# Key and value products on four quarter tiles of TensorE, in a four-block convolution and attention kernel

## The reference

```python
qkv = xf @ qkv_w.T + qkv_b                  # xf: (B, N, 64), N = 128*128 pixels
q, k, v = ...                               # 8 heads of 8 channels each
k = _layernorm(k, kln_w, kln_b)             # over the 8 channels of a head, std with ddof=1
v = _layernorm(v, vln_w, vln_b)
kv = einsum('bhnd,bhne->bhde', k, v) / N    # sum over all pixels
av = einsum('bhnd,bhde->bhne', q, kv)
h1 = gelu((av + x) @ o1_w.T + o1_b)
out = h1 @ o2_w.T + o2_b + x
```

## Time and profile before

| | us |
|---|---|
| median of three executions | 2690.85 (2689.84 to 2691.07) |
| profiled execution | 2696.16 |
| its span | 2694.4 |
| TensorE matmul busy | 2546.2 (95%) |
| TensorE weight loads busy | 2460.3 (91%) |
| VectorE busy | 1848.3 (69%) |
| ScalarE busy | 1220.0 (45%) |
| GpSimd busy | 171.3 (6%) |
| mean granted TensorE clock | 0.979 |

### The profile page before, as it was taken

How to read it: one execution, slowest core, us unless ns; L and a number is a source line. 1 busy time by engine, 2 the same in 40 slices (tenths; PEclk the granted TensorE clock), 3 DMA queues, 4 the chain that set the end, 5 groups by cost and what they waited for, 6 DMA issues and landing times.

```text
span 2694.4 us, 115786 instructions
## 1 busy us (share of the span) xinstructions
PE 2546.2 (95%) x45062; PEld 2460.3 (91%) x45062; DVE 1848.3 (69%) x6030; ACT 1220.0 (45%) x2531; POOL 171.3 (6%) x291
## 2 busy tenths in 40 slices
PE   1999999999999999997899999999999999978998
PEld 1299999999999999997899999999999999977985
DVE  7866666666566666678566666666666666787876
ACT  0866663222233333356666632222333333566767
POOL 1610000000000000000000000000000000002435
PEclk9999999999999999998899999999999999988999
DMA  6810001222300000024900012224000000240006
GB/s 262 223 32 0 0 0 45 60 61 59 94 0 0 0 5 0 0 65 115 368 17 0 0 38 60 62 60 101 0 0 0 0 0 0 63 110 16 3 2 250
DMA packets 158376, 146.46 MB, mean 54 GB/s; under 512 B 22497, under 2 KB 146018, under 8 KB 154210
## 3 DMA queue, kind: packets, MB, share of 16 engines
q1 hardware_dynamic: 146432, 142.65, 17.8%
q10 hardware_dynamic: 11874, 2.90, 0.5%
HBM read 61.61 MB, written 50.33 MB: 42 GB/s over the span
## 4 chain that ended last, share of the span: by engine, by line
PE 91%; DVE 3%; DMA 3%; issue 2%; SPq 1%; ACT 1%; DVEq 0%; ACTq 0%; POOL 0%
PE banks L750 82%; PE banks L804 4%; PE banks L816 1%; PE banks L723 1%; PE banks L712 1%; DMA state<-x_in 1%; PE banks L797 1%; DVE state L950 1%; DMA res<-resid 1%; SPq L265 1%; DVE state L1086 0%; DMA resid<-state 0%; DVE state L947 0%; ACTq L465 0%; DMA state<-resid 0%
## 5 line engine op out<-in xcount | busy, mean ns | idle before, releaser
L750 PE MATMUL banks<-x_row,w_taps 128*64 128x124 f32 (+2 forms) x40640 | 2207.7, 270 | 16.6 <-DVE x_row L1000 9.1
L750 PEld LDWEIGHTS banks<-x_row,w_taps 128*64 128x64 f32 x40640 | 2205.3, 135 | 18.9 <-issue 9.8
L1009 DVE SCALAR_TENSOR_TENSOR x_row<-banks,sweep_nbias,biased_row 128x128 f32<-128x128 f32 x2032 | 714.2, 351 | 723.2 <-PE banks L750 704.0
L552 ACT ACTIVATE biased_row<-state,sweep_bias 128x256 f32 (+1 forms) x762 | 511.2, 671 | 1029.3 <-DVE state L1012 594.5
L548 ACT ACTIVATE biased_row<-state,aff,gn_a 128x64 f32 (+1 forms) x1016 | 364.1, 429 | 185.1 <-DVE state L1018 185.1
L1012 DVE SCALAR_TENSOR_TENSOR state<-banks,sweep_nbias,biased_row 128x128 f32 (+1 forms) x1016 | 444.1, 437 | 0.3
L1018 DVE SCALAR_TENSOR_TENSOR turn_ring<-banks,sweep_nbias,biased_row 128x64 f32<-128x64 f32 x1016 | 237.5, 276 | 0.0
L1018 DVE SCALAR_TENSOR_TENSOR state<-banks,sweep_nbias,biased_row 128x64 f32 (+1 forms) x1016 | 237.4, 276 | 0.1
L410 POOL TENSOR_SCALAR res<-res 128x128 f32<-128x128 f32 x64 | 43.2, 675 | 2397.1 <-ACT res L661 2397.0
L804 PEld LDWEIGHTS banks<-kvw_s,state 64*128 64x128 f32 x1024 | 118.1, 308 | 0.1
L723 PE MATMUL banks<-res,ffn_w 64*64 64x512 f32 x512 | 112.3, 597 | 6.0 <-ACT res L484 5.2
(11 more groups left out here) (137 smaller groups left out, 777.0 us busy)
## 6 DMA issues: line engine op xcount, KB each, us to landing
state<-turn_ring SPq DMA_DIRECT2D x512, 64.0 KB, 1.9
state<-x_in SPq DMA_DIRECT2D x16, 1024.0 KB, 20.7
resid<-state SPq DMA_DIRECT2D x64, 256.0 KB, 3.7
res<-resid SPq DMA_DIRECT2D x16, 1024.0 KB, 9.1
res<-resid SPq DMA_DIRECT2D x32, 512.0 KB, 5.4
resid<-state SPq DMA_DIRECT2D x16, 1024.0 KB, 11.6
out_y<-state SPq DMA_DIRECT2D x16, 1024.0 KB, 4.0
state<-resid SPq DMA_DIRECT2D x32, 256.0 KB, 9.2
```

What stands on the lines that cost most here:

```text
L552: nc.scalar.activation(as_cells(n, biased_row[:, k, :, :]), cells(n, slice(0, B), i, k, g), ACT.Identity, bias=sweep_bias[:, n:n + 1]).the ...
L750: last = nc.tensor.matmul(out_ps[blk, :, lo:hi], w_taps[:, n % 2, s, blk], x_row[c][src][:, :, s + lo:s + hi], start=at == 0, stop=at == T ...
L1009: nc.vector.scalar_tensor_tensor(x_row[c][par][:, :, 2:2 + HALF], ps, nb, br, ALU.max, ALU.add).then_inc(row_ready[c], 1)
```

## The change

Each matmul of line 804 with 128 weight columns (pixels) becomes two with 64 weight columns, one for each half m of the pixels, which write partitions 0 to 63 and 64 to 127 of the same bank. With the two halves q that makes four quarter tiles of the array (64 rows x 64 columns). The moving operand, the banks, the sums, their order over t and the semaphores stay. The bias products of line 797 and everything else stay as they are. (The feed-forward before and after is the same in both kernels.)

```diff
                     for q in range(2):
                         blk = slice(q * C, (q + 1) * C)
                         col = q * BANK + t * KVN
-                        last = nc.tensor.matmul(pair[n % KV_BANKS][:, col:col + KVN], half_rows[blk, top:top + P, b, w],
-                                                kvw_s[blk, b, :], start=False, stop=t == PARTS - 1)
+                        for m in range(2):
+                            at = slice(m * C, (m + 1) * C)
+                            last = nc.tensor.matmul(pair[n % KV_BANKS][at, col:col + KVN],
+                                                    half_rows[blk, top + m * C:top + (m + 1) * C, b, w],
+                                                    kvw_s[blk, b, :], start=False, stop=t == PARTS - 1)
                 last.then_inc(kv_done, 1)
```

## The result

| | before | after |
|---|---|---|
| median, us | 2690.35 (4 executions) | 2669.02 (4 executions, 2666.94 to 2671.62) |
| ratio | | 0.9921, 95% interval 0.9904 to 0.9939 |
| profiled execution, us | 2696.16 | 2671.62 |
| its span, us | 2694.4 | 2669.8 |
| first bias load of the loop to the last reduce, us | 170.5 | 146.4 |

The change is faster by 21.3 us; 28.5 were forecast. The last row of the table cuts out the loop, from the first weight load of line 797 to the start of line 1135's last reduce, and is the cleanest measure of the change. What lies ahead of the loop is the same code in both, yet its length differs from one execution to the next: the loop started between 2437.3 and 2444.5 us in the profiles of this study. What lies behind it took 79.4 us before and 79.5 after.

What follows compares the result with a forecast made beforehand. TensorE was taken to bound the attention loop, with VectorE next at 2.185 us a tile. Gains of 28.1 us in the loop and 0.4 at start-up, 28.5 off the median 2690.85, gave 2662.4 us, range 2657 to 2676.

Steps and rivals of the forecast that it cites:

- What bounds the kernel: Attention loop: TensorE never idle for 158.4 us, 2.68 us a tile; only shortening its part moves the time.
- Why 804 was slow: Key/value products: weight loads of the two row tiles go one after the other, 0.22 us a round, about twice streaming.
- Step 1: Line 804's products: loads hide behind streaming, eight rounds of 0.099 us, 0.79 us a tile in place of 1.65.
- Step 2: Tile-shape switches between 797, 804 and 816: still two a tile, one moves; cost 0 to 0.2 us, taken as 0.
- Step 3: TensorE's tile after the change: 0.41 + 0.79 + 0.62 = 1.82 us, or 2.02 with a further switch.
- Step 4: Next bound in the loop: VectorE sets the tile at 2.185 us, TensorE waiting about 0.3 us a tile.
- that case (2668): VectorE's tile in the loop 2.26 us instead of 2.185, from a product of 0.77 for 0.69; costs 4.5 us.
- Step 5: The sum: 28.1 us from tile 6's reduce to the last, 0.4 at start-up, 0 behind the loop; 28.5 us.
- Serial loads: Rival on 804: 32 loads one after another take 1.76 us; 2691 us, or 2704 with 0.2 more a tile; 5%.
- The clock: Rival: waiting TensorE drops to clock 0.50, its tile 3.4 us; 2732 us if the whole loop ran so; 4%.
- Loads not hidden behind streaming: Rival on 804: round 0.15 us, 804 takes 1.2, TensorE's tile 2.2 to 2.43; up to 2676 us; 7%.
- the sign that was to overturn the forecast: The forecast fails altogether if TensorE's matmul row stays full over the loop.

Runs made afterwards that it cites:

- half the columns: Changed kernel with each key/value product streaming 56 of its 112 columns; round 0.147 us, one execution 2667.0 us.
- the control: The changed kernel run once more, nothing altered; 2666.99 us, ratio 0.991 to the kernel before.
- GpSimd later: Changed kernel with dense weights, GpSimd's two steps for tile n held until VectorE has scaled tile n - 2; 2662.63 us, ratio 0.9907.
- GpSimd later alone: Changed kernel with its true weights, only GpSimd's steps held until VectorE has scaled tile n - 2; 2666.82 us, ratio 0.9913.

## Why the prediction was right, and where not

**What bounds the kernel.** Right: TensorE's share of the tile was the bound, and shortening 804 moved the time. The two small engines behind it were not.

**Why 804 was slow.** Wrong in its reason. The loads were the limit, as read, but I took the earlier trace rows (lone dense loads of 0.11 us) and the earlier trace rows (pairs of 0.22) to show that loads of two row tiles are serial. The runs show that they are parallel, and that the stride of 512 bytes took the time: 0.112 us a round with dense weights in the old form. The comparison that hid it was between a lone dense tile and a strided pair; two things differed at once, and I named only one. I even wrote that the stride has no price, on that ground. The records of the kernel before held the answer: the two loads of a round start 0.003 us apart and last 0.310 us each, and the next two start 0.220 us later. The earlier trace rows shows them merged.

**Step 1, loads and streaming.** The term of the sum that was mis-sized: 0.79 us for 806 was expected, 8 x 0.147 = 1.18 measured. The interpolation itself was good: with dense weights the round is 0.096 where 0.099 was worked out, and TensorE's tile less its wait is 2.261 - 0.452 = 1.81 us where 1.82 was forecast. The gram's row was the wrong price because its weights are dense. I had the doubt in the text (four strided loads at once may have a price), gave it 7%, and put the right size (0.15) on it, but with another mechanism: half the columns show that no streaming is in these 0.147 us.

**Step 2, switches.** Right. The gap moved from the gram to 806. Measured between the same points, the way from the bias load to the second round of the products grew by 0.21 us, and that from the last round of the products to the gram's second round shrank by 0.22.

**Step 3, TensorE's tile.** 1.82 forecast, 2.24 measured: 0.39 of the difference is step 1.

**Step 4, what is late next.** Half right. VectorE is next and free of waits, as the earlier trace rows foretold at 2.185 us, but for a TensorE faster than that the tile is 2.26, since GpSimd's step then meets the product. The range had that case (2668) from the product of 0.77 in the earlier trace rows; the sum didn't. The Trainium skill, "SBUF — State Buffer", Who interferes with whom, says that a VectorE instruction with two inputs in SBUF contends with a GpSimd one that reads there, and calls the contention an exclusive lock. The traces agree that the two contend. As for the lock, they agree where VectorE comes first (410 takes 1.11 us, held until the product's end); where GpSimd comes first, they show only 0.08 us of delay beside a step of 0.66.

**Step 5, the sum.** From the reduce of tile 6 to the last one 127.2 us were measured (2463.19 to 2590.36) for 124.5 forecast: 2.7 us of the miss. The two mistakes on the tile partly hid each other: with the round at 0.099 the tile would have been 2.26, and the gain smaller still. The start lost instead of gaining: a gain of 0.4 was expected. The reduce of tile 6 came 19.2 us after the first bias load, 17.9 before; 0.9 of that is the late clock of that execution. The rest lies in the first tiles, as these rows show (first tile, clock 0.50):

```profile
2444.63 1.47 PEld L806 LDWEIGHTS banks<-kvw_s,state 64*64 64x64 f32 x32 [0.38 <-issue]
...
2446.37 0.29 PEld L797 LDWEIGHTS banks<-bias_rows,picks 64*128 64x128 f32 x2 [0.27 <-issue]
```

The loads take 1.47 us where they took 2.01, and a round is 0.187 where 0.198 was worked out for this clock, but gaps of 0.38 and 0.27 stand ahead of them and behind them. While no gram products run between the tiles, the switches are not moved but added, two a tile; the prediction had taken off only some 0.2 us for them in both tiles together. From first bias load to the next bias load the tile took 2.41 us, 0.34 more than before (2.07). With an early clock (the control) the loop was 145.5 us, 25.0 shorter than before, against 28.5 forecast. The miss of the median, 2669.0 against 2662.4, adds up from two parts. Profile against profile the gain was 24.5 us for 28.5 (4.0). The other 2.7 are the 5.3 us by which the profiled execution of the kernel before lay over its median, which I carried over whole: the one after lay 2.6 over its own.

**The rivals.** Serial loads did not occur: the round fell from 0.220 to 0.147. The clock, once it had risen at 2454.3 us, stayed at 1.00 to the loop's end, and it did so as well in the kernels where TensorE waits 0.37 to 0.45 us a tile (dense weights, without and with GpSimd later; 1.00 from 2456 to 2575 us). The one fall inside a loop came in its first tiles, in the kernel before with dense weights. Loads not hidden behind streaming: its size came nearly true, by another cause.

**Luck.** That the time came out within the range is in part luck. TensorE's tile of 2.24 us happens to lie 0.06 above VectorE's 2.185, so a term that was wrong by half of its size cost 3 us. The engine that was forecast to bind did not, and the sign that was to overturn the forecast, TensorE's full row, did appear.

## What to carry to other kernels

When a weight load is the limit, look first at how its operand lies in memory: with weights 512 bytes apart a round of 128-column loads took 0.220 us, with adjacent ones 0.112. More tiles of the array got back a part of that (0.147), no more. Price a new form from a row that has the same operand layout as well as the same shape; if no row has both, the two differences need a price each. And when an engine is freed, check which step of a third engine will now fall beside the next bound: here a free change of GpSimd's timing was worth 0.08 us a tile, as soon as TensorE was no longer the bound.

## What the runs showed of the hardware that was not expected

- Weight loads of 64 columns on four quarter tiles: 0.096 us a round at 4 and 8 bytes, 0.114 at 128, 0.119 at 516, 0.147 at 512 (there it doesn't change when half the columns are streamed). On two row tiles of 128 columns: 0.112 dense, 0.220 at 512 bytes.
- The loads of two row tiles run side by side: two dense ones of 128 columns pass in 0.112 us, as a lone one does, and two at a stride of 512 bytes start 0.003 us apart.
- Beside the quarter loads at 512 bytes other engines' steps got longer. ScalarE's copy (666) and GpSimd's 410, first in the changed kernel, then with dense weights, both over 2460 to 2580 us:

```profile
L666 ACT ACTIVATE res<-banks 128x896 f32<-128x896 f32 x54 | 53.4, 988 | 0.0
...
L410 POOL TENSOR_SCALAR res<-res 128x128 f32<-128x128 f32 x54 | 40.5, 750 | 53.0 <-ACT res L661 53.0
```

```profile
L666 ACT ACTIVATE res<-banks 128x896 f32<-128x896 f32 x53 | 47.9, 903 | 0.0
...
L1150 DVE TENSOR_TENSOR res<-res 128x512 f32<-128x512 f32 x53 | 40.9, 771 | 1.8
...
L410 POOL TENSOR_SCALAR res<-res 128x128 f32<-128x128 f32 x53 | 35.1, 661 | 58.0 <-ACT res L661 58.0
```

  At 128 and 516 bytes the copy took 0.904 and 0.909, and in the kernel before, with 512 bytes on two row tiles, 0.911. GpSimd's 410 took 0.750 in the changed kernel and 0.661 with dense weights, but a part of that is its meetings with the product. Two runs have none in the middle of the loop, GpSimd later alone and with dense weights (here it is line 412, and it runs beside the reduce in both, 2460 to 2570 us):

```profile
L412 POOL TENSOR_SCALAR res<-res 128x128 f32<-128x128 f32 x49 | 34.6, 707 | 50.0 <-ACT res L663 50.0
```

```profile
L412 POOL TENSOR_SCALAR res<-res 128x128 f32<-128x128 f32 x51 | 33.6, 659 | 52.4 <-ACT res L663 50.3 <-issue 2.0
```

  So some 0.05 us of it go with the strided quarter loads. What they share with these steps is not shown.
- VectorE's product of two operands in SBUF takes 0.77 to 0.80 us when it starts behind a GpSimd step and 0.69 alone; a GpSimd step that starts behind the product is held until its end (1.11 us for 0.66).
- When the granted clock returns to 1.00 after the loop's start differs by 7 us and more between executions of like kernels (2.7 to 10.3 us, once 30); between the two profiles of the changed kernel this goes with a difference of 0.9 us at the reduce of tile 6.
